# Loading TensorE's expert numbers five at a time, and adding the down bias last, in a four-stage pipelined vision tower on Trainium2

## What is computed

```python
h = _L0_tok_ref(x, ...)                  # depthwise 3x3 convolution, 8x8 mean: 64 tokens per image
h = h + _L0_attn_ref(_layernorm(h), ...) # attention inside one image
h = h + _L0_ffn_ref(_layernorm(h), ...)
...
def _L0_ffn_ref(x, gate_w, gate_b, sw1, sb1, sw2, sb2, rw1, rb1, rw2, rb2):
    B, S, D, F, E, NS, K = (2, 512, 128, 512, 8, 2, 2)
    hs = gelu(einsum('td,nfd->ntf', t, sw1) + sb1)          # two shared experts, every token
    shared = einsum('ntf,ndf->td', hs, sw2) + sb2.sum(axis=0)
    probs = softmax(t @ gate_w.T + gate_b)
    top_v, top_i = top_k(probs, K)                          # two of eight routed experts per token
    hr = gelu(einsum('td,efd->etf', t, rw1) + rb1)
    oe = einsum('etf,edf->etd', hr, rw2) + rb2
    return shared + routed                                  # oe weighted by top_v and summed
...
h = h + _L1_attn_ref(_layernorm(h), ...) # rotary attention with compressed keys
h = h + _L1_ffn_ref(_layernorm(h), ...)  # two triangular products over the channels
```

## Time and profile before

| | us |
|---|---|
| median of 3 runs | 2091.96 |
| lowest, highest | 2079.8, 2095.05 |
| the profiled execution | 2071.78 |
| its span in the trace | 2070.0 |
| PE busy in the span | 1745.7 (84%) |
| weight loads (PEld) busy | 1352.3 (65%) |
| DVE busy | 1268.4 (61%) |
| ACT, POOL busy | 948.9, 950.9 (46% each) |

### The profile page before, as it was taken

The page is one execution under the profiler, slowest core; times in us unless marked ns, Lnnn a source line. Parts: engine busy times, 40 slices in busy tenths (PEclk is TensorE's granted clock), DMA queues, the critical chain, the costliest instruction groups (busy, mean ns, idle before and its releaser), DMA issues.

```text
span 2070.0 us, 47437 instructions
## 1 busy us (share of the span) xinstructions
PE 1745.7 (84%) x15216; PEld 1352.3 (65%) x15216; DVE 1268.4 (61%) x3484; ACT 948.9 (46%) x2291; POOL 950.9 (46%) x770
## 2 busy tenths in 40 slices
PE   1454879989897989899897989899897989998956
PEld 1443766868676776768676776768675776866644
DVE  2566456757675766767575766767675756753432
ACT  0122534546463645456363635445463635553522
POOL 1224245454556555464456464464445554533222
PEclk9999988989999999999898989999998989999986
DMA  6647454544544444545445444544445444301000
GB/s 245 243 163 255 179 201 167 194 154 152 203 183 168 181 168 175 199 148 192 157 178 204 181 155 155 211 158 172 165 168 209 179 136 170 131 20 50 17 26 6
DMA packets 109170, 332.08 MB, mean 160 GB/s; under 512 B 13662, under 2 KB 87585, under 8 KB 92412
## 3 DMA queue, kind: packets, MB, share of 16 engines
q1 hardware_dynamic: 86416, 300.90, 39.5%
q0 software_dynamic: 8992, 19.42, 2.9%
q10 hardware_dynamic: 13516, 8.51, 1.4%
HBM read 299.48 MB, written 29.29 MB: 159 GB/s over the span
## 4 chain that ended last, share of the span: by engine, by line
PE 65%; POOL 10%; issue 9%; DMA 7%; DVE 4%; ACT 2%; ACTq 1%; SPq 1%; POOLq 0%; DVEq 0%
PE hid_bank L598 11%; PE pool_bank L452 6%; DMA outs_d<-ys 5%; PE pool_bank L457 5%; POOL yg L1357 5%; PE sec_bank L654 4%; PE hid_bank L583 4%; PE sec_bank L674 4%; PE hid_bank L582 3%; PE sec_bank L665 3%; POOL xbuf L1346 3%; PE hid_bank L584 2%; PE sec_bank L617 2%; PE sec_bank L634 2%; PE down_bank L543 2%
## 5 line engine op out<-in xcount | busy, mean ns | idle before, releaser
L1346 POOL TENSOR_TENSOR xbuf<-xbuf 128x512 f32<-128x512 f32 x256 | 330.1, 1289 | 528.3 <-DVE xbuf L1039 518.5
L850 ACT ACTIVATE hid<-hid_bank,bias_t 128x128 f32<-128x128 f32 x960 | 273.7, 371 | 122.3 <-PE hid_bank L584 116.4
L598 PE MATMUL hid_bank<-w_s,hid 128*128 x1920 | 291.3, 297 | 0.0
L598 PEld LDWEIGHTS hid_bank<-w_s,hid 128*128 128x128 f32 x1920 | 243.8, 199 | 16.7
L1039 DVE TENSOR_TENSOR xbuf<-xbuf 128x1536 f32<-128x1536 f32 x128 | 236.7, 1849 | 25.9 <-DMA xbuf<-in_x 25.9
L582 PE MATMUL hid_bank<-xt,w_b 128*128 128x128 bf16 x960 | 201.3, 230 | 33.8 <-issue 18.4
L1060 DVE SCALAR_TENSOR_TENSOR taps<-pooled_s,tapw,taps 128x256 f32<-128x256 f32 (+1 forms) x416 | 210.0, 505 | 29.9 <-issue 21.6
L1043 DVE TENSOR_TENSOR xbuf<-xbuf 128x512 bf16<-128x512 f32 x128 | 90.3, 706 | 213.5 <-ACT xbuf L764 213.4
L1384 POOL TENSOR_TENSOR keys_h<-keys,heads 128x632 f32<-128x632 f32 x128 | 198.6, 1578 | 18.1 <-PE sec_bank L654 15.6
L1200 DVE COPY ys<-hid_bank 128x128 f32<-128x128 f32 x240 | 68.8, 287 | 219.0 <-PE hid_bank L598 192.8
L583 PE MATMUL hid_bank<-xt,w_b 128*128 128x128 bf16 x960 | 202.9, 230 | 0.1
(11 more groups left out here) (213 smaller groups left out, 3443.7 us busy)
## 6 DMA issues: line engine op xcount, KB each, us to landing
xbuf<-in_x SPq DMA_DIRECT2D x128, 2048.0 KB
rows_s<-rows_d SPq DMA_DIRECT2D x48, 320.0 KB, 8.9
outs_d<-ys SPq DMA_DIRECT2D x240, 64.0 KB
out<-h ACTq DMA_DIRECT2D x16, 256.0 KB
w_s<-in_w ACTq DMA_DIRECT2D x1, 2560.0 KB
hid<-in_w POOLq DMA_DIRECT2D x10, 256.0 KB, 3.7
rows_d<-x2r,spot_i POOLq DMA_INDIRECT x128
yg<-outs_d,spot_i POOLq DMA_INDIRECT x128
```

The costliest lines, as they stand in the source:

```text
L598: mm = nc.tensor.matmul(hid_bank[n % 2][:, 0:P], hid[:, n % RING, q * P:(q + 1) * P], w_q, start=False, stop=q == FC - 1)
L850: ins = nc.scalar.activation(hid[:, n % RING, cols], hid_bank[n % 2][:, cols], ACT.Gelu, bias=bias_t[:, q, j:j + 1])
L1346: nc.gpsimd.tensor_tensor(v[:, :, 1, :], v[:, :, 1, :], v[:, :, 2 * k + 3, :], ALU.add) \
```

## The change

A new piece `aim` k loads the expert numbers of rows 5k to 5k+4 (AIMED = 5) into registers and keeps all of them in `held`. It stands three times in TensorE's list: aim.0 behind att.2 and ahead of lift.0, aim.1 behind pre.4 and ahead of pool.1.1, aim.2 behind pool.2.3 and ahead of turn.3. `widen` and `narrow` only look the register up. aim.0 first waits for the router's last step of that group (which `table`, earlier in the block, has waited for as well) and increments a semaphore that nobody reads. In `narrow` the four fp32 products now come first (`start` at the first) and the bias matmul last (`stop=True`, and it carries the semaphore).

```diff
+AIMED = 5
...
-        pool.0.2 up.7 down.5 down.6 att.1 down.7 att.2 lift.0 pool.0.3 lift.1 widen.0 widen.1 lift.2 att.3
+        pool.0.2 up.7 down.5 down.6 att.1 down.7 att.2 aim.0 lift.0 pool.0.3 lift.1 widen.0 widen.1 lift.2 att.3
...
+            def aim(g, b, k):
+
+                if k == 0:
+                    eng.wait_ge(gate_step, at(gate_step, g, 28))
+                    eng.sem_inc(table_in, 1)
+                for j in range(k * AIMED, (k + 1) * AIMED):
+                    held[j] = eng.value_load(owner_i[b][0:1, j:j + 1], min_val=0, max_val=NE - 1)
+
+            def owner_of(b, j):
+
+                if j not in held:
+                    held[j] = eng.value_load(owner_i[b][0:1, j:j + 1], min_val=0, max_val=NE - 1)
+                return held[j]
...
             def widen(g, b, j):
...
-                e = held[j] = eng.value_load(owner_i[b][0:1, j:j + 1], min_val=0, max_val=NE - 1)
+                e = owner_of(b, j)
                 eng.wait_ge(lift_ready, at(lift_ready, g, j + 1))
...
             def narrow(g, b, j):
...
-                e = held.pop(j, None)
-                if e is None:
-                    e = eng.value_load(owner_i[b][0:1, j:j + 1], min_val=0, max_val=NE - 1)
+                e = owner_of(b, j)
                 eng.wait_ge(hid_made, at(hid_made, g, n + 1))
-                nc.tensor.matmul(hid_bank[n % 2][:, 0:P], owned[b][0:3 * NE, j:j + 1].to_broadcast([3 * NE, P]),
-                                 bias_b[0:3 * NE, F:F + C], start=True, stop=False)
                 for q in range(FC):
                     w_q = w2_s[:, bass.ds(e + NS, 1), q * P:(q + 1) * P].rearrange("p a c -> p (a c)")
-                    mm = nc.tensor.matmul(hid_bank[n % 2][:, 0:P], hid[:, n % RING, q * P:(q + 1) * P], w_q,
-                                          start=False, stop=q == FC - 1)
+                    nc.tensor.matmul(hid_bank[n % 2][:, 0:P], hid[:, n % RING, q * P:(q + 1) * P], w_q,
+                                     start=q == 0, stop=False)
+                mm = nc.tensor.matmul(hid_bank[n % 2][:, 0:P], owned[b][0:3 * NE, j:j + 1].to_broadcast([3 * NE, P]),
+                                      bias_b[0:3 * NE, F:F + C], start=False, stop=True)
                 mm.then_inc(hid_used, 1)
```

More of the change, by code:

```diff
@@ L48 @@
                 att="att", low="att", high="att", rest="att", scatter="att", up="ffn", hidden="ffn", down="ffn", moe="ffn",
-                rows="ffn", table="ffn", lift="ffn", widen="ffn", narrow="ffn", store="ffn",
+                rows="ffn", table="ffn", aim="ffn", lift="ffn", widen="ffn", narrow="ffn", store="ffn",
                 gate="ffn", load="tok", keep="set", gather="sec", mix="sec", pre="sec",
@@ L62 @@
         up.0 up.1 table up.2 down.0 up.3 down.1 up.4 up.5 down.2 out' up.6 down.3 down.4 pool.0.0 pool.0.1
-        pool.0.2 up.7 down.5 down.6 att.1 down.7 att.2 lift.0 pool.0.3 lift.1 widen.0 widen.1 lift.2 att.3
[L64 to L71, removed]
+        pool.0.2 up.7 down.5 down.6 att.1 down.7 att.2 aim.0 lift.0 pool.0.3 lift.1 widen.0 widen.1 lift.2 att.3
+        narrow.0 pre.2 narrow.1 lift.3 widen.2 att.4 pre.3 lift.4 narrow.2 lift.5 pool.1.0 pre.4 aim.1 pool.1.1
+        widen.3 pre.5 pre.6 pre.7 widen.4 narrow.3 score.0 pool.1.2 score.1 pool.1.3 lift.6 att.7 score.2 score.3
+        widen.5 lift.7 score.4 score.5 narrow.4 score.6 score.7 att.8 widen.6 lift.8 narrow.5 turn.0 widen.7
+        turn.1 lift.9 value.0 pool.2.0 pool.2.1 narrow.6 turn.2 pool.2.2 widen.8 value.1 lift.10 pool.2.3 aim.2
+        turn.3 lift.11 value.2 narrow.7 turn.4 value.3 att.10 widen.9 turn.5 narrow.8 value.4 att.11 turn.6
+        value.5 narrow.9 turn.7 widen.10 lift.12 value.6 widen.11 lift.13 value.7 narrow.10 pool.3.0 att.12
+        post.0 narrow.11 post.1 widen.12 lift.14 pool.3.1 widen.13 narrow.12 pool.3.2 widen.14 pool.3.3 narrow.13
+        narrow.14 post.3 post.4 post.5""",
     act="""
@@ L708, in experts @@
                     table(g, b)
+                elif kind == "aim":
+                    aim(g, b, j)
                 elif kind == "lift":
```

## The result

The changed kernel took 2162.12 us (median of 4 runs, 2155.28 to 2165.92), the kernel before 2085.88 beside it (4 runs, 2076.43 to 2095.05). The ratio is 1.036, 95% interval 1.030 to 1.042: 76 us slower. The prediction was 2152, in a range of 2108 to 2186.

What follows compares the result with a forecast made beforehand. The prediction took TensorE, 65% of the chain, as the bound. Aims +1.0, +1.0, +2.3, freed loads -0.85 and bias +0.6 sum to 4.05 us a block, 61 us over 15 blocks: forecast 2152, range 2108 to 2186.

Steps and rivals of the forecast that it cites:

- The band that the prediction calls likeliest: Time, 2138 to 2165: 0.6 us a load takes 0.75 off a block, no bias term 0.6; bias at 1.0 adds 0.4.
- A load in a row costs 0.65 us: At each aim, five loads in a row take 5 x 0.65 = 3.25 us of sequencer, plus 0.1 for the added wait.
- Rival B: At the aims, loads in a row cost about 0.30 us each; -0.3 us a block, 2087, no change; chance 0.12.
- The three holes: The array stalls ahead of lift.0 by +2.3 us, pool.1.1 by +1.0 and turn.3 by +2.3 in each block.
- Rival A: At the aims, loads are covered and all gaps close; 22 us gained, time 2070; chance 0.05.
- the sequencer's lead over the array: At aim.1 and aim.2, leads of 2.4 and 1.1 us cover only part of the 3.25 us of loads.
- forecast net +1.0: At aim.0, lift.0 comes 2.3 us later and lift.2 regains 1.3 from two missing loads: net +1.0 us a block.
- The bias last, +0.6 a block: In narrow, entering the 24-row weight load behind fp32 pieces costs 0.19 us each; +0.6 us a block, between 0 and 1.0.
- That all of the delay reaches the end: All three load places lie inside TensorE's stretch of the chain, so a delay there moves everything behind and the next block.
- the freed loads: At widen.11 and widen.9, loads no longer made there give back 0.85 us a block; widen.12 to 14 give 0.
- rival D: At the aims, another engine's nearly as long chain absorbs delays, costs may halve: 30 us, time 2122; chance 0.13.
- Rival C: Over the block, the clock pays on top: 5.7 us a block, 85 us, time 2177; chance 0.2.

Runs made afterwards that it cites:

- the filled kernel: Changed kernel plus unread 512-column products, nine ahead of aim.2's loads and three ahead of value.6: 2125.5 us, 1.019 of the kernel before.
- the aims only: Kernel before with the loads moved to aim.0, aim.1 and aim.2, bias matmul still first in narrow: 2157.5 us, 1.036 of before.
- bias last alone: Kernel before with only the bias matmul moved last in narrow, every widen loading its own number: 2063.9 us, 0.991 of before.
- the fillers: Unread 512-column products put where the array idles, added to three kernels: aim.1 only 2099.7 us, aim.2 only 2104.9, the changed kernel 2125.5.
- aim.1 alone: Kernel before with only rows 5 to 9 loaded between pre.4 and pool.1.1, bias first: 2149.4 us, 1.031 of before.
- aim.2 alone: Kernel before with only rows 10 to 14 loaded between pool.2.3 and turn.3, bias first: 2151.5 us, 1.034 of before.
- aim.0 alone: Kernel before with only rows 0 to 4 loaded between att.2 and lift.0, bias first: 2125.1 us, 1.017 of before.

## Why the prediction was right, and where its account was not

**The sum held by luck in part.** Forecast: 61 us, all of it delay. Measured: 76 us, of which 37 (the filled kernel) to 45 (the split by the clock) are delay, and the rest is clock. The delay was taken a third to two thirds too high, and the clock was in no term of the sum. The two errors have opposite signs. The band that the prediction calls likeliest, 2138 to 2165, doesn't follow from the terms that it names either: they take off 1.35 us a block and add 0.4, which gives 2132 to 2158, and the measured 2162 lies just above it.

**A load in a row costs 0.65 us:** right, 0.64 to 0.70 by the groups of five. No run times a semaphore check alone; the 0.1 us for it was an estimate. Rival B falls, and with it the idea that the next load overlaps the register operations of the last.

**The three holes:** right to 0.1 us, means of ten blocks. From att.2's first weight load to lift.0's 1.21 us before, 3.52 after: +2.31, forecast +2.3. From pre.4's last to pool.1.1's first 0.43 and 1.54: +1.1, forecast +1.0. From pool.2.3's last to turn.3's first 0.04 and 2.34: +2.3, forecast +2.3. Rival A falls. What the step rests on, that the sequencer's lead over the array is 1.1 to 2.4 us there, holds: from an aim's first load to the weight load behind it pass 3.3 us at all three places (936.3 to 939.59, 954.4 to 957.70, 990.9 to 994.18), and 1.1 us of them show as added spacing at aim.1, 2.3 at aim.2. That a wait stops it is seen at aim.0: its first load starts at 936.3, behind att.2's weight load at 936.10, which had waited for ACT's copy (to 936.05). widen.2 comes 0.95 us later after att.2 with the aims only and 1.3 in the changed kernel, forecast net +1.0. The first weight loads of widen.0, 1 and 11 came 0.59, 0.99 and 0.45 us after the one ahead of them and now come 0.10, 0.11 and 0.17 after it.

**The bias last, +0.6 a block:** as a delay of the array about right. By the spacings it is +0.8: the entries behind fp32 pieces, lifts and widens cost what the prediction said, and so does narrow.0, where the 24-row load waits longest (0.95 us) but a 128-row one gains nothing by coming sooner. As a term of the time it failed: bias last alone was 26 us faster where +9 was forecast, and the term has no place for what an edit does to the clock (0.921 to 0.935).

**That all of the delay reaches the end:** only in part. In the filled kernel, where half-clock time is as before, narrow.7's products start 3.7 us later after att.2 than before, value.6 3.6, att.12 2.9, and the period is 2.8 longer, not 4.05. What goes between value.6 and att.12 are the freed loads (-0.85 in the sum). So hardly anything is absorbed from narrow.7 on, and rival D's mechanism, another engine's chain that is nearly as long, isn't seen there. What is missing lies ahead of it: of 1.0, 1.0 and 2.3 us for the three aims, 0.5 show from att.2 to widen.2, 0.8 on to widen.3, and 2.4 on to narrow.7, the last with 0.2 to 0.4 of bias in it. Why the first is only half, when it was 0.95 without the fillers, isn't known.

**Rival C**, the clock on top, is what the changed kernel shows at aim.2, where the granted clock was 0.50 from between 1.1 us before turn.3 and 2.0 us after it. It reckons with 5.7 us a block, 1.65 more than the forecast's 4.05, which was my estimate for one new stretch; no run shows what one stretch costs, and the upper end of the range, 2186, rests on it. The runs showed 7.9 us more half-clock time a block and a period of 121.1 against 115.3 us; the 121.1 is of one profiled run, and the kernel before is on the fast side in its own. I gave C 0.2. It deserved more: the trace of before had 15.1 us at half clock a block already (the earlier trace rows is one such stretch), so the stretches had to be in the sum for every hole, and every hole moved. And I looked for the new stretch only behind the new hole. The runs of aim.0 and aim.1 alone show it 50 (aim.1) to 65 us (aim.0) further on, at a hole that another engine's fixed order makes once TensorE comes there at full clock.

**Open.** Why the short stretch at turn.7 is there in some kernels and blocks and the long one behind value.6 in others can't be told from here; neither can it be foreseen which of two similar kernels gets the better pattern. The fillers show that the holes are a cause, not that they are the only one: in eight of ten blocks the kernel before falls to half clock in turn.7 with no idle time over 0.2 us in the 10 us ahead of it.

## What to carry over

Price a stall of TensorE at its own length and at the half-clock stretch that may stand behind it, here or at a later hole. In this kernel, with 15.1 us at half clock a block, an edit that delayed by 0.9 us lengthened the block by 5.0 (aim.1 alone), and one that delayed by 0.8 made the kernel 26 us faster (bias last only, mean granted clock 0.921 to 0.935), so an edit has to be judged with the mean granted clock beside its time. Register loads belong where the array waits for another engine anyway, and only those that are not covered: four loads ahead of att.1 gained 45 us, five behind att.2, pre.4 or pool.2.3 lost 40 to 65. Unread products in an unavoidable hole are a cheap test of whether the clock is the price, and sometimes a remedy: they took aim.1's loss from 65 us to 8.

## What the runs showed of the hardware

- Behind some idle stretches of TensorE the granted clock fell to 0.50, and behind others not. Ahead of turn.3 (2.1 to 2.2 us idle in the changed kernel, 2.2 to 2.4 with aim.2 alone) a half-clock stretch of 3.4 to 10.2 us began between 1.1 us before turn.3's first weight load and 2.0 us after it, in all of ten blocks of either. Ahead of value.6 with aim.1 alone (0.9 to 1.4 us idle) one of 6.8 or 10.2 us began 1.2 to 3.3 us behind it, in all of ten. Ahead of pool.1.1 in the changed kernel (1.3 to 1.4 us idle) none began within 20 us, in none of ten; holes of 0.6 to 0.9 us in three blocks of aim.0 alone and one of 1.1 us in the kernel before had none either.
- With unread products in the hole, 0.4 to 0.6 us of it were left ahead of value.6 and 1.0 to 1.1 ahead of turn.3, and half-clock time fell from 21.9 to 13.7 us a block (aim.1) and from 22.2 to 15.0 (aim.2).
- Behind an fp32 product of 512 columns a weight load of 24 rows comes 0.95 us after the product's second weight load, one of 128 rows 0.43 us after it and the next another 0.43 later. With 128 rows in place of 24 the bias matmul takes 0.14 to 0.25 us less in each narrow at full clock.
- Loads of a register from SBUF in a row start 0.64 to 0.70 us apart on TensorE's sequencer, by the groups of five, with their register operations and assertions between them: the fifth 2.56 to 2.79 us behind the first, where one TENSOR_LOAD lasts 0.30 us (L578 of the changed kernel).
